# Layer 1's input copied first, sums ahead of choices, prefix behind layer 3, taps placed by the host

## The reference, cut to what matters

```python
out = x                                   # (128 samples, 32 channels, 512)
for i, typ in enumerate(('same', 'upsample', 'same', 'downsample')):
    s = style @ mod_w[i].T + mod_b[i]                     # per sample, per input channel
    weight = SCALE * weights[i] * s[:, None, :, None]
    weight = weight * rsqrt(sum(weight**2, axis=(2, 3)) + EPS)
    out = conv3(out, weight, typ) + biases[i]             # with a (1,3,3,1) blur around up and down
h = out.reshape(4096, 512)
scores = sigmoid(h @ gate_w.T) + bias                     # 16 experts
topk_w, topk_idx = top_k(scores, 4); topk_w = topk_w / sum(topk_w)
moe = sum over the 4 chosen experts e of topk_w[e] * (silu(h @ Wg[e].T) * (h @ Wu[e].T)) @ Wd[e].T
result = x + moe + (silu(h @ Sg.T) * (h @ Su.T)) @ Sd.T   # the shared expert
```

## Time and profile before

| | |
|---|---|
| median of 3 runs | 1250.92 us (1247.87 to 1251.91) |
| profiled execution | 1250.38 us, of which the span of the trace is 1248.7 us |
| PE busy over the span | 1139.2 us (91%) |
| DVE, POOL, ACT busy | 804.7 us (64%), 574.0 us (46%), 501.1 us (40%) |
| PE busy in slices of a fortieth, in tenths | 3699999999999898765999999999999999999995 |

### The profile page before, as it was taken

One profiled execution on the slowest core, in us unless ns is written; L12 is line 12 of the kernel. 1 busy time (PEld: TensorE's weight loads), 2 busy tenths in 40 slices (PEclk: granted clock), 3 DMA queues, 4 the chain that ended last, 5 costly groups with the idle time before them and its releaser, 6 DMA issues. The chain is left out here.

```text
span 1248.7 us, 24559 instructions
## 1 busy us (share of the span) xinstructions
PE 1139.2 (91%) x7160; PEld 1002.9 (80%) x7161; DVE 804.7 (64%) x1979; ACT 501.1 (40%) x1164; POOL 574.0 (46%) x667
## 2 busy tenths in 40 slices
PE   3699999999999898765999999999999999999995
PEld 2477777777777777644999999999998899999995
DVE  6556777777777777655565565656557665555653
ACT  4455555655555555322232332333233332222321
POOL 1000151424233332364665656566656566666663
PEclk9999999999999998966999999999999999999998
DMA  4455444454444453214767676676766776665664
GB/s 148 128 177 144 136 135 138 135 148 135 135 135 141 131 140 110 77 34 135 158 124 151 112 154 124 152 118 117 155 115 159 186 142 136 115 113 109 114 112 74
DMA packets 141626, 162.43 MB, mean 130 GB/s; under 512 B 33120, under 2 KB 98720, under 8 KB 140064
## 3 DMA queue, kind: packets, MB, share of 16 engines
q0 software_dynamic: 35696, 74.34, 32.6%
q1 hardware_dynamic: 104608, 87.78, 23.8%
q10 hardware_dynamic: 1296, 0.01, 0.1%
HBM read 73.41 MB, written 55.18 MB: 103 GB/s over the span
## 5 line engine op out<-in xcount | busy, mean ns | idle before, releaser
L1253 PE MATMUL bank<-xt_hi,wup_hi 128*128 128x256 f32 x1104 | 275.4, 282 | 1.8 <-issue 1.7
L1253 PE MATMUL bank<-xt_hi,wup_lo 128*128 128x256 f32 x1104 | 275.1, 282 | 0.0
L477 POOL DMA_INDIRECT out_rows<-yb,sid x140 | 226.5, 1618 | 91.7 <-DVE yb L1036 68.5
L418 POOL DMA_INDIRECT lists<-entry,place x128 | 129.1, 1009 | 237.3 <-DVE place L863 188.6
L560 ACT ACTIVATE t<-bank,cB,cA 128x256 f32<-128x256 f32 (+1 forms) x384 | 173.9, 530 | 116.1 <-PE bank L217 112.9
L1253 PEld LDWEIGHTS bank<-xt_hi,wup_hi 128*128 128x128 f32 x1104 | 209.4, 190 | 6.5 <-issue 3.7
L1253 PEld LDWEIGHTS bank<-xt_hi,wup_lo 128*128 128x128 f32 x1104 | 208.9, 189 | 2.7
L464 POOL DMA_INDIRECT xg<-h_rows,gid x140 | 142.3, 1016 | 120.3 <-PE bank L1231 76.7
L1257 PE MATMUL bank<-xt_lo,wup_hi 128*128 128x256 f32 x1104 | 176.2, 281 | 0.0
L1036 DVE TENSOR_SCALAR yb<-bank,all_lists 128x512 f32<-128x512 f32 x138 | 100.0, 748 | 85.2 <-DMA out_rows<-yb,sid 51.0
L1257 PEld LDWEIGHTS bank<-xt_lo,wup_hi 128*128 128x128 f32 x1104 | 150.9, 189 | 0.0
(11 more groups left out here) (212 smaller groups left out, 2182.9 us busy)
## 6 DMA issues: line engine op xcount, KB each, us to landing
x<-x1p SPq DMA_DIRECT2D x64, 384.0 KB
wraw<-in_Wup SPq DMA_DIRECT2D x11, 1024.0 KB, 7.4
xraw<-in_xq SPq DMA_DIRECT2D x32, 260.0 KB, 3.9
xbase<-in_x SPq DMA_DIRECT2D x32, 256.0 KB, 2.7
h_rows<-hrow SPq DMA_DIRECT2D x128, 64.0 KB, 1.7
out_rows<-orow SPq DMA_DIRECT2D x32, 256.0 KB, 2.1
x<-x1p SPq DMA_DIRECT2D x64, 127.0 KB
wdraw<-in_Wdn SPq DMA_DIRECT2D x11, 512.0 KB, 9.5
```

The lines of the kernel that those rows point to most:

```text
L418: pool.indirect_dma_start(out=lists, out_offset=bass.IndirectOffsetOnAxis(ap=place[:, home, r, k:k + 1], axis=0), in_=entry[:, home, r, k, ...
L477: pool.indirect_dma_start(out=out, out_offset=bass.IndirectOffsetOnAxis(ap=sid[:, u:u + 1], axis=0), in_=yb[:, u, :], in_offset=None, comp ...
L1253: pe.matmul(dst, lhs[a], rhs[0], start=k == 0 and a == 0, stop=False)
```

## The change

1. **Taps placed by the host.** The block matrices come ready from the host as `placed` (20 matrices of 128x128, 1.3 MB, in three DMAs). Those of layers 0 and 2 are split as they are; up and down are mixed out of 4 and 12 matrices by eight DVE instructions (`mixture`), behind the first scales and around x1p of group 0. `big`, `mats`, the function `matrices` and PE's 11 transposes are gone; the sums of squares are taken from `wtap` on 32 partitions; nine small DMAs for biases become one.
2. **Set-up order.** On POOL the first two `scaled` stand in front of the wait for the fill writes (L407). PE's layer 0 of group 0 waits for one matrix, not for all; the second part of the scales, some constants and the gate's split come behind it.
3. **Layer 1's input first.** DVE makes x1p of group g+1 at the start of body g, in front of x2. On SP `stack(g + 1)` comes in front of the `h_rows` writes and the load of `xraw` behind them.
4. **Sums in front of choices.** `settle` is cut in two. Its first part (up to `pos`) stays in the body, behind `z`; its second part, now `places`, and `choose` and `mark` come behind `orow` in conv bodies (`routing`). Behind the last conv body they stand earlier, behind `z`.
5. **Prefix behind layer 3.** PE's prefix counts, and so the wait for `mask`, move from in front of layer 1 to behind layer 3. PE's transposes of `z` wait for `pos`, not for `place`.
6. **64-byte lines.** Behind a buffer whose size is 1 to 32 bytes over a multiple of 64, 32 bytes are left empty.

```diff
...
+            buffer = ctx.enter_context(nc.sbuf_tensor(name, shape, dt))
+            size = 2 if dt == BF16 else 4
+            for n in shape[1:]:
+                size *= n
+            if 0 < size % 64 <= 32:
+                ctx.enter_context(nc.sbuf_tensor(f"{name}_gap", [P, 8], F32))
...
-            for q in range(Q):
-                sp.dma_start(wnat[C * q:C * q + C].rearrange("o l i k -> o l (i k)"),
-                             cw.rearrange("l o i k -> o l (i k)")).then_inc(S["taps_loaded"], 16)
             sp.dma_start(xraw[:, 0], xq[0]).then_inc(S["x_loaded0"], 16)
+            sp.dma_start(placed[:, PLACED_UP:PLACED_DOWN], placed_taps[:, PLACED_UP:PLACED_DOWN]).then_inc(S["placed_loaded1"], 16)
+            sp.dma_start(placed[:, PLACED_DOWN:], placed_taps[:, PLACED_DOWN:]).then_inc(S["placed_loaded2"], 16)
...
                 odd = g % 2 if u is None else (R + 1 + u) % 2
-                if within(g, 0, G - 3):
...
                 if within(g, 3, G + 3):
...
+                if within(g, 0, G - 1):
+                    stack(g + 1)
                 if within(g, 1, G + 1):
                     sp.wait_ge(S["h_ready"], g)
...
-                if within(g, 0, G - 1):
-                    stack(g + 1)
+                if within(g, 0, G - 3):
+                    sp.wait_ge(S["x0_hi"], g + 2)
+                    sp.wait_ge(S["x0_lo"], g + 2)
+                    sp.dma_start(xraw[:, 1 - odd], xq[bass.ds(g + 3, 1)].rearrange("a p b v -> p (a b) v")).then_inc(S[f"x_loaded{1 - odd}"], 16)
...
+            pool.wait_ge(S["s_ready"], 1)
+            for g in range(2):
+                scaled(g, g % 2, g // 2)
             pool.wait_ge(S["fill_written"], 16 * 2)
...
+            for g in range(2, 2 * R):
...
+            act.dma_start(smalls[:], small).then_inc(S["bias_loaded"], 16)
+            act.dma_start(wtap[:].rearrange("i l o k -> i (l o k)"), taps.rearrange("i l o k -> i (l o k)")).then_inc(S["taps_loaded"], 16)
+            act.dma_start(placed[:, 0:PLACED_UP], placed_taps[:, 0:PLACED_UP]).then_inc(S["placed_loaded0"], 16)
+            def matrix_hi(n):
+                src, at, to, m = MATRICES[n]
+                act.activation(cwt[0][:, to:to + m], src[:, at:at + m], ACT.Copy).then_inc(S["wts_hi"], 1)
+            act.wait_ge(S["placed_loaded0"], 16)
+            for n in range(2):
+                matrix_hi(n)
...
+            act.wait_ge(S["scales_ready"], 1)
+            layer0(0)
+            for n in range(2, 4):
+                act.wait_ge(S["mixed_ready"], n - 1)
+                matrix_hi(n)
+            first_in(1, 1)
...
+            dve.wait_ge(S["taps_loaded"], 16)
...
+            dve.wait_ge(S["s_psum"], 1)
+            dve.wait_ge(S["bias_loaded"], 16)
+            link(dve.tensor_tensor(s[:], bank[4][:].rearrange("p (l b) -> p l b", l=NL),
...
+            dve.memset(tsum[:], 0.0).then_inc(S["s_ready"], 1)
+            dve.tensor_tensor(s2[:], s[:], s[:], ALU.mult).then_inc(S["s2_ready"], 1)
+            def matrix_lo(n):
+                src, at, to, m = MATRICES[n]
+                dve.wait_ge(S["wts_hi"], n + 1)
+                minus(cwt[1][:, to:to + m], src[:, at:at + m], cwt[0][:, to:to + m]).then_inc(S["wts_lo"], 1)
...
+            for n in range(2):
+                matrix_lo(n)
+            first_in(0, 0)
...
+            def mixture(to, m, at, weights, sem_name):
+                dve.wait_ge(S[sem_name], 16)
+                for n, weight in enumerate(weights):
+                    term = placed[:, at + n * m:at + n * m + m].rearrange("p t m -> p (t m)")
+                    mix = mixed[:, to:to + m].rearrange("p t m -> p (t m)")
+                    if n == 0:
+                        r = dve.tensor_scalar(mix, term, weight, None, ALU.mult)
+                    else:
+                        r = dve.scalar_tensor_tensor(out=mix, in0=term, scalar=weight, in1=mix, op0=ALU.mult, op1=ALU.add)
+                    if n < len(weights) - 1:
+                        link(r)
+                r.then_inc(S["mixed_ready"], 1)
+            mixture(0, 1, PLACED_UP, UPK, "placed_loaded1")
+            layer0(0)
+            mixture(1, 3, PLACED_DOWN, BK, "placed_loaded2")
+            for n in range(2, 4):
+                matrix_lo(n)
+            link(inverse(2))
...
-                step(dve.tensor_tensor(pos[:, 0:many], bank[7][:, 0:many * E].rearrange("p (r e) -> p r e", r=many),
-                                       every(region[:], many), ALU.add))
+                dve.tensor_tensor(pos[:, 0:many], bank[7][:, 0:many * E].rearrange("p (r e) -> p r e", r=many),
+                                  every(region[:], many), ALU.add).then_inc(S["pos_ready"], 1)
+            def places(number, home, many):
+                dve.wait_ge(S["pos_ready"], number)
...
+                def gathered():
+                    if stage:
+                        dve.wait_ge(S["logits_done"], g - 1)
...
+                def routing():
+                    if many:
+                        places(number, 2 if many == R else (number - ROUNDS - 1) % 2, many)
+                    if stage and early and g > LAST:
...
+                    elif not early and u == 0:
+                        choose(it + 1, R)
+                    elif not early and u == 1:
+                        mark(2, ("scattered", it * (16 * TOPK * R) + 16), R)
+                if within(g, 0, G - 1):
+                    layer0(g + 1)
...
-                if within(g, 0, G - 1):
-                    layer0(g + 1)
-                many, number = settled(g, it, u)
-                if many:
-                    settle(number, 2 if many == R else (number - ROUNDS - 1) % 2, many)
                 if stage:
                     dve.wait_ge(S["sg_ready"], g - 1)
...
+                if many:
+                    settle(number, many)
+                if not conv:
+                    gathered()
+                    routing()
                 if within(g, 0, G - 2):
                     first_in(g + 2, odd)
...
-                if stage:
-                    dve.wait_ge(S["logits_done"], g - 1)
...
-                elif not early and u == 0:
-                    choose(it + 1, R)
-                elif not early and u == 1:
-                    mark(2, ("scattered", it * (16 * TOPK * R) + 16), R)
+                if conv:
+                    gathered()
                 if stage:
                     dve.wait_ge(S["down_done"], g - 1)
...
                     dve.tensor_tensor(orow[:, odd, :], xbase[:, odd, :], bank[5][:], ALU.add).then_inc(S["o_ready"], 1)
+                if conv:
+                    routing()
...
                 if within(g, 0, G - 1):
                     layer0(g + 1)
-                many, number = settled(g, it, u)
-                if many:
-                    pe.wait_ge(S["mask_ready"], number)
-                    pe.wait_ge(S["zt_lo"], g - 2)
...
-                    ins.then_inc(S["prefix_done"], 1)
...
+                many, number = settled(g, it, u)
+                if many:
+                    pe.wait_ge(S["mask_ready"], number)
...
+                    def logits():
...
+                    if not conv:
+                        logits()
                     pe.wait_ge(S["z_ready"], g - 1)
                     if many:
-                        pe.wait_ge(S["place_ready"], number)
+                        pe.wait_ge(S["pos_ready"], number)
                     turn_z(0, bank[7]).then_inc(S["zt_t"], 1)
...
+                    if conv:
+                        logits()
...
```

More of the change, by code:

```diff
@@ L33, in mk_adaln_ffn @@
     PAD = 2 * P
[L34 to L39, removed]
+    FIRST, SAME, UP, DOWN, NM = 0, 2, 4, 5, 8
     Q = P // C
@@ L248, in routed @@
                             one()
[L251 to L273, removed]
+        MATRICES = ((placed, 0, FIRST, 2), (placed, 2, SAME, 2), (mixed, 0, UP, 1), (mixed, 1, DOWN, 3))
         def within(g, least, most):
@@ L817, in choose @@
                 dve.wait_ge(S["sig_ready"], number)
-                step(dve.tensor_tensor(sc[:, 0:many], sig[:, 0:many], every(biasrow[:], many), ALU.add))
+                step(dve.tensor_tensor(sc[:, 0:many], sig[:, 0:many], every(biasrow, many), ALU.add))
                 land(dve)
@@ L1160, in body @@
                     lo_passes(pe, dst, terms).then_inc(S["l3_done"], 1)
+                many, number = settled(g, it, u)
+                if many:
+                    pe.wait_ge(S["mask_ready"], number)
+                    pe.wait_ge(S["zt_lo"], g - 2)
+                    pe.matmul(bank[7][:, 0:many * E], tri[:], mask[:, 0:many], start=True, stop=False)
+                    for r in range(many):
+                        if r:
+                            pe.matmul(bank[7][:, r * E:many * E], ones[:], mask[:, 0:many - r], start=False, stop=False)
+                        ins = pe.matmul(bank[7][:, r * E:r * E + E], ones[:], mask[:, R], start=False, stop=r == many - 1)
+                    ins.then_inc(S["prefix_done"], 1)
```

(16 more changed lines are left out.)

204 lines of the change are left out of this document (74 added, 130 removed).

## The result

The changed kernel takes 1262.0 us (median of four runs, 1260.8 to 1263.1), the kernel before 1250.7 beside it: a ratio of 1.0069, 95% interval 1.0039 to 1.0099. So it is slower by 0.7%, 11 us, where I had forecast 1252 and 1246 to 1258. That is inside the wide range, 1238 to 1268, and outside the likeliest case's own.

A forecast was written before the change was run, and what follows sets the result against it. PE was taken to bound the conv loop, matmuls the expert phase, a chain the set-up. 1250.4 - 18.9 (set-up) + 20.7 (loop) - 0.4 (behind it) = 1251.8, forecast 1252 us; likeliest 1246 to 1258, wide range 1238 to 1268.

The forecast's parts named there:

- wide range: Whole kernel: 1238 to 1268 us, leaving out about 0.2 of the chance.
- likeliest case: Whole kernel: 1252 us, own range 1246 to 1258, chance 0.48.
- Set-up: Start of the kernel up to body 5: earlier scaling, weights and copies of x1 gain 18.9 us, 14 to 21.
- The stall: One loop body of four: late `place` delays scaling and zt_hi; PE idles 4.9 us, loses 1.35 to clock; body 20.9 us.
- The other bodies: The three loop bodies of each round without the new wait: 14.3, 14.55 and 14.55 us.
- "pure" body: A conv loop body of the kernel before without stalls, taken as 14.15 us.
- Behind the loop: Last bodies up to the experts: 6.7 us less, 6.3 more for late scatters; net 0.4 gained, between 4 lost and 4 gained.
- 64-byte lines: Buffer addresses in SBUF: no effect on the time taken.
- Cover holds: Rival, loop: scaling of group 4 it + 10 done before ACT needs it, loop gains 16.8 us: 1214 us, chance 0.15.
- the rival's 11 to 13: Rival, set-up: larger loads hold things up or body 2 keeps its wait; gain 11 to 13 us, about 1259, chance 0.12.
- The clock: Rival, loop: PE keeps its clock over the six new waits, 8.1 us less: 1244 us, chance 0.13.
- The ports: Rival, loop: each of POOL's eight scatters waits for one DVE instruction of 0.42 us, six rounds: 1272 us, chance 0.12.

The follow-up runs named there:

- e4: The kernel before with only x1p first in DVE's body and, on SP, copies of x1 ahead of the h_rows writes, loads of x last: 1253.0 us.
- e9: e5 with the first two scalings behind POOL's wait for the fill writes again, as before the change: 1249.4 us, one run on another chip.
- e1: The changed kernel with POOL's scaling of group 4 it + 10 in front of the wait for `place` instead of behind two sets of scatters: 1235.8 us.
- e1b: The changed kernel with POOL's scaling of group 4 it + 10 behind one set of four scatters instead of two: 1233.0 us in one run.
- e2: The changed kernel with `places` directly behind `settle` in conv bodies instead of behind orow, POOL's order kept: 1229.8 us.
- e3: The changed kernel without the 32-byte gaps between buffers: 1263.0 us.
- e7: e1 with POOL's scaling of group 4 it + 11 behind the second set of scatters instead of the third: 1230.3 us, on another chip.
- e8: e5 with xt_hi on ACT and xt_lo on DVE between the two halves of layer 1's output instead of behind both: 1203.9 us.
- e6: e1 with PE's prefix counts back in front of layer 1: 1257.8 us in one run.
- e10: e8 with the routing constants and low parts of the shared expert's weights moved behind body 0 on DVE: 1205.7 us.
- e11: e5 with `choose` and `mark` in front of orow again: ratio 0.973 to the kernel before, on a chip where that kernel was 31 us slower.
- e5: The changed kernel with `settle` and `places` in front of z, in DVE's wait for ACT's sigmoid: 1219.4 us.

## Why the prediction was right and wrong

The time lies in the wide range, but the likeliest case missed it by 10 us: the set-up gave 2.4 us less than forecast, the loop lost 10.7 more, and the stretch behind it gave 2.4 more.

- *Set-up.* The scaling started at 8.39 (forecast 7.3), the reciprocals at 12.48 (11.1), the weight splits at 26.30 (25.3), layer 1 at 27.91 (26.2). Some 1.1 us of delay ran through from the scaling, and the copies weren't there at 23 but at 27.9, 10 us behind the end of x1p (17.66) instead of 6.6. That the larger loads held them is likely and not shown. At layer 1 of body 2 I had 16.4 us and it was 14.2 (64.58 to 50.37): 2.26 us of wait for copies stayed. From there to body 5 came 2.3 us more, forecast 2.55. Sum 16.5 for 18.9. e4 and e9 divide it: copies first 7.5, scaling in front of the fill wait 10.4, together 17.9, more than the 16.5. But body 5 stood anywhere from 92.75 to 95.88 us in e1, e1b, e2, e3 and e7, whose set-up is that of after. What the matrices made by the host are worth stays open, as no run has them alone.
- *The stall.* It was in the right body, by the right chain, six times. That its size was right was luck, by two errors: idle 4.25 us instead of 4.9, and the lower clock some 2.3 us (21.26 - 14.64 - 4.33; 2.1 by the busy times of after and e1) instead of 1.35. The one precedent had 2.7 us at the lower level, here it was 3 to 5. The body took 21.1 us on average, forecast 20.9.
- *The other bodies: the step that failed.* I put them at 14.3, 14.55 and 14.55 us and they took 14.6, 15.2 and 15.3: 45.0 a round instead of 43.4, 9.7 us in all, which is nearly the whole miss of the loop. I had taken a "pure" body as the length less the wait I saw, 14.15. But behind the waits for copies and `mask` stood others, for xt_hi and xt_lo, late by nearly as much. The loop of before had 1.7 us of these, that of after has 11.5. So of the 15.1 us of waits for copies and `mask` 9.8 came back under those names. e4 shows for the copies alone that taking away a wait gave nothing, there mostly by orow and `mask`. That `places` and x1p ahead of x2 on DVE make xt_lo late, by up to 0.7 us, is my reading of the order, and not tested apart. And a wait cost more than its shown length, as e8 tells: the length less the shown waits isn't a body without waits. e8's ordinary body took 13.82 us, under my 14.15.
- *Behind the loop.* -2.8 for -0.4. From the end of the last z (556.99) to the end of the last scatter (574.58) it took 17.6 us, forecast 18.2; up to that z the bodies took 8.5 us less instead of 6.7. How much of it is the prefix's isn't shown: e6's 12.6 us there hold for `mark` behind orow.
- *64-byte lines.* Nothing in the time, as forecast (e3).
- *The rivals.* "Cover holds" would have given 1214; with the stall away e1 has 1236, so its price too was worked out from the bodies that failed. The set-up gave 16.5 us, nearer to the forecast than to the rival's 11 to 13. The clock did fall behind each of the six stalls (granted 0.50 to 0.69 over the 5 us behind). "The ports" came out in another form. In body 8 of after no scatter was held (1.27 us apart but for the first). In e1 and e7 it is POOL's scaling that holds and DVE that waits, some 1.3 us a time. The rule of the Trainium skill (SBUF — State Buffer, SBUF: two separate sides) has this case too: an exclusive lock on the shared pair of ports, between DVE in a two-port form, or with two inputs in SBUF, and a GpSimd operation, in the second case one that reads SBUF. I had told only of the two-port forms. The traces agree as to the operands: the additions that were held read t and edge, both in SBUF, and `logit` and orow, which kept their length, read PSUM. Which of the two took the ports first they don't show: in e1 the addition is recorded from 154.49 and the scaling from 154.84, and yet the addition waits. I had weighed the wrong instruction of POOL's and the wrong loser.

## What to carry to other kernels

Before a step is moved, list what is queued behind its wait on every engine that takes it in: one wait for `place` held a scaling that didn't need it. A wait that is removed is worth only the distance to the next one late; look for that by taking the order of ACT's and DVE's work in one body, since there, and not in the longest wait, lay the gain of e8. And where an operation of one engine holds up another engine, as POOL's scaling does DVE, it should run where nobody waits for the other: moving it was worth 5.5 us (e1, e7).

## What I had not expected of the hardware

A short idle piece can cost more than its length. In e10's trace PE stood still for 2.14 us with no releaser shown. The granted clock, 1.00 up to 261 us, was 0.71 in the next microsecond and 0.50 from 262 to 271, and the body took 20.74 us instead of 14.8:

```profile
261.66 0.34 PE L214 MATMUL bank<-x_hi,cwt_hi 128*128 128x4 f32 x1 [2.14 <-issue]
```

```profile
252.00:260.00 8.00, 7.52 (x38) 1.00 0.73 180
260.00:274.00 14.00, 12.34 (x45) 0.63 0.28 71
```

That is 3.8 us of clock for 2.1 of idle time, against 2.1 to 2.3 for 4.3 in the stalls of after. And chips differ more than executions: the kernel before took 1247 to 1257 us on two and 1280 to 1290 on the third, where such pieces with no releaser added up to 4.3 and 4.8 us in the loops of e9 and e11. They aren't the reason as far as can be seen: e8's loop on that chip has none, and e1b's and e5's on the other two have 1.5 and 1.2 us.
